# Layer 3's aggregate of a graph network on one core: groups of eight tiles and a ring of 32 gathers

## The chip, the core and the metric

The kernel runs on one core of a Trainium2 chip. The core has TensorE (PE, matrix products; its weight loads are listed as PEld), VectorE (DVE), ScalarE (ACT), GpSimd (POOL) and SyncE (SP), each with a program of its own; they meet only through semaphores. The metric is the time on the device of one execution of the whole kernel, in microseconds. TensorE's clock has two levels, 1.2 and 2.4 GHz; the profile gives the granted clock as a share of the upper one.

## The reference

The model has four layers, each with a graph part and a feed-forward part, on 3125 nodes with 256 features and 50000 edges. The change touches the graph part of the last layer:

```python
def _L3_gnn_ref(node_repr, weight, bias, edge_index, edge_types):
    h_all = jnp.einsum('ni,roi->rno', node_repr, weight)      # 8 relations
    src, dst = (edge_index[0], edge_index[1])
    msgs = h_all[edge_types, src]                             # 50000 rows of 256
    messages = jax.ops.segment_sum(msgs, dst, num_segments=node_repr.shape[0])
    return messages + bias
...
x = x + _L3_gnn_ref(_layernorm(x, axis=-1), L3_gnn_weight, L3_gnn_bias, edge_index, edge_type_8)
x = x + _L3_ffn_ref(_layernorm(x, axis=-1)[None], ...)
```

## The kernel before

A stage ahead of this one has written `h_all` as a table of 8 x 3125 rows to HBM (`g.relations`), and the edges have been sorted by their destination and cut into ST = 416 tiles of 128 edges, so that all edges of a tile go to nodes of one block of 125 (there are T = 25 blocks). The tile's block number is in `g.kmap`; an edge's row in the table and its place in the block are in `g.slots`. The sum over edges of tile n is then

- a gather (GpSimd, line 915): 128 rows of 1 KB of the table to `got[:, n % 16, :]`, an indirect DMA whose landing counts the semaphore `gathered[n % 16]` up by 16;
- a one-hot matrix (VectorE, line 935): 128 edges by 125 places, made for four tiles at a time (`QUAD`), written to `hot`, with the semaphore `hot_ready`;
- a product (TensorE, line 928): `hot` turned, times `got`, 125 x 256 values in one half of a PSUM bank. It stands as two records in the trace. Every second tile counts `multiplied` up;
- an addition (VectorE, line 954) of the product to the block's rows of X, whose place is a register loaded from `g.kmap`. Every second tile counts `added` up.

The order on each engine is that of the loops over n. GpSimd has 16 places: from gather 16 on, it waits ahead of every second gather for `multiplied` of the tiles 16 places back. TensorE waits for each gather's landing, for the one-hots of its four tiles, and from tile 16 on for `added`, since PSUM holds 16 products (8 banks of two). VectorE makes the one-hots of tiles n+8 to n+11 before it adds the products of tiles n to n+3, and waits for `multiplied` ahead of each addition. ScalarE has turned the indices into integers before the first gather, and SyncE has nothing to do, since the list `loads` is empty.

The stage stands by itself between two barriers in which all semaphores that are free are cleared. Behind it follows the last feed-forward part (`layer3_ffn`, lines 2376 to 2608), which reads X.

In the printed order of instructions semaphores have the first name that their number was given: same_loaded0 is `multiplied`, same_loaded1 is `added`, deg_opened is `hot_ready`, deg_hot_used is `staged`, and moved0 to moved15 are `gathered`. In the same way the profile calls a wait for number 141 (`multiplied`) sometimes by an early DMA, edges_other, that used the number first.

## Time and profile before

| | us |
|---|---|
| median of 3 runs | 4360.08 (4359.11 to 4368.43) |
| the profiled execution | 4384.73 |
| its span, first to last instruction | 4383.0 |
| the stage of the change, 3349.2 to 3950.2 us of the span: GpSimd busy | 405.1, 416 gathers |
| TensorE busy in it | 341.7, 832 records |
| VectorE busy in it | 175.5 for 416 additions, 70.6 for 104 one-hots |

The rows further down come from the views of this profile. A row of instructions reads: line, engine, operation, what is written <- what is read, shapes, count, busy time and mean, and behind a second bar the idle time of the engine ahead of them with what ended it. "issue" means that the profile shows nothing that the engine waited for.

### The profile page before, as it was taken

To read this page: it belongs to the slowest core of one execution; us is meant where nothing else is said; L and a number is where in the kernel's file an instruction comes from. 1 tells how busy PE (TensorE), PEld (TensorE's weight loads), DVE (VectorE), ACT (ScalarE), POOL (GpSimd) and SP (SyncE) were. 2 spreads that over 40 slices of the span, in tenths; PEclk is the share of its full clock that TensorE was granted. 3 is DMA by queue.
4 is the path that set the end of the run, shared out by engine and by line. 5 is a ranking of instruction groups with operands and counts; after the bars stand their busy time and mean duration, and the time that the engine had idled before them with its cause. 6 is when DMAs were issued, how large, how long until landed. Compare 5 with 4: busy or idle time off the path is not lost. (4 is left out here: it accounts for less than half of the span.)

```text
span 4383.0 us, 52512 instructions
## 1 busy us (share of the span) xinstructions
PE 3195.9 (73%) x17915; PEld 2449.1 (56%) x17916; DVE 1390.7 (32%) x3307; ACT 804.2 (18%) x2090; POOL 2275.9 (52%) x1830
## 2 busy tenths in 40 slices
PE   0999955574999993596089999968697555553993
PEld 0555543454999993596078878855443333332562
DVE  3333355442441114011621111133432434442005
ACT  0666622211000001232121100023200000001220
POOL 5587777775666666765236656600002666662003
PEclk9999977777999995798599999969897666665996
DMA  8663222228999886699133333300143333332222
GB/s 338 233 191 84 4 6 6 11 8 246 276 286 276 253 233 156 156 245 228 42 127 133 134 119 131 107 15 0 39 140 123 91 91 92 93 90 75 98 90 69
DMA packets 368093, 562.71 MB, mean 128 GB/s; under 512 B 177053, under 2 KB 246493, under 8 KB 351584
## 3 DMA queue, kind: packets, MB, share of 16 engines
q1 hardware_dynamic: 201740, 393.74, 28.0%
q0 software_dynamic: 158320, 122.06, 15.2%
q10 hardware_dynamic: 7824, 44.20, 2.5%
q8 instruction: 122, 2.00, 0.2%
q14 instruction: 87, 0.71, 0.0%
HBM read 413.40 MB, written 145.88 MB: 128 GB/s over the span
## 5 line engine op out<-in xcount | busy, mean ns | idle before, releaser
L455 POOL DMA_INDIRECT count_cells<-cells_count,added_row x391 | 645.4, 1651 | 282.8 <-issue 119.4
L874 POOL DMA_INDIRECT weight_cells<-added_weight,added_row x391 | 610.2, 1561 | 321.2 <-DMA weight_cells<-added_weight,added_row 181.4
L915 POOL DMA_INDIRECT g3g_got<-relations,g3g_idx x416 | 405.1, 974 | 685.7 <-ACTq L86 498.2
L1429 PE MATMUL g_acc<-XN,g_blocks 125*125 125x128 f32 x5000 | 567.8, 275 | 55.0 <-DMA g_blocks<-count_cells 52.6
L1429 PEld LDWEIGHTS g_acc<-XN,g_blocks 125*125 125x125 f32 x5000 | 559.6, 189 | 59.6 <-issue 52.8
L1742 PE MATMUL g_acc<-g_H,g_blocks 125*125 125x256 f32 x2500 | 557.6, 382 | 23.8 <-DMA g_blocks<-weight_cells 13.2
L1659 POOL DMA_INDIRECT slots_dram<-sort_rec,sort_row x392 | 379.8, 969 | 349.0 <-issue 112.5
L928 PE MATMUL g3g_pp<-g3g_got,g3g_hot 128*125 128x256 f32 x832 | 341.7, 560 | 271.4 <-issue 205.8
L1742 PEld LDWEIGHTS g_acc<-g_H,g_blocks 125*125 125x125 f32 x2500 | 471.4, 189 | 102.5 <-issue 31.8
L928 PEld LDWEIGHTS g3g_pp<-g3g_got,g3g_hot 128*125 128x125 f32 x832 | 203.8, 270 | 409.5 <-issue 247.8
L954 DVE TENSOR_TENSOR X<-X,g3g_pp 125x256 f32 x416 | 175.5, 422 | 349.2 <-DMA edges_other<-digits_dram 183.7
L723 ACT ACTIVATE same_same<-same_scores 128x128 bf16<-128x128 f32 (+7 forms) x392 | 255.1, 651 | 145.5 <-PE same_scores L712 129.0
L708 PE MATMUL same_scores<-edges_other,edges_own 11*128 11x512 bf16 (+2 forms) x490 | 206.9, 483 | 22.5 <-ACT same_same L723 21.5
L1786 DVE SCALAR_TENSOR_TENSOR g_tmp<-g_acc,dinv,g_b 125x256 f32<-125x256 f32 x50 | 24.2, 484 | 506.8 <-PE g_acc L1742 250.6
L2582 POOL DMA_INDIRECT f3y_Y<-results,f_back x25 | 35.6, 1426 | 273.7 <-PEq L86 266.3
L1869 PE MATMUL g_psO<-g_w,g_xT 128*125 128x512 f32 x400 | 173.8, 596 | 0.0
L1450 ACT ACTIVATE g_uT<-g_psT 128x125 f32<-128x125 f32 (+1 forms) x75 | 20.6, 275 | 627.3 <-PE g_psT L1404 528.7
L2117 PEld LDWEIGHTS f1e_pH<-XN,f1e_w 128*128 128x128 f32 x1040 | 128.2, 194 | 3.8 <-issue 0.4
L2139 PE MATMUL f1e_pY<-w,XN 128*128 x512 | 123.0, 384 | 10.0 <-issue 10.0
L2117 PE MATMUL f1e_pH<-XN,f1e_w 128*128 128x128 f32 x1040 | 128.5, 278 | 0.0
L1869 PEld LDWEIGHTS g_psO<-g_w,g_xT 128*125 128x125 f32 x400 | 75.4, 189 | 94.9 <-issue 94.9
L710 PE MATMUL same_scores<-edges_other,edges_own 11*128 11x128 bf16 x392 | 119.9, 306 | 8.1 <-DMA edges_other<-digits_dram 8.1
(624 smaller groups left out, 4530.4 us busy)
## 6 DMA issues: line engine op xcount, KB each, us to landing
g_blocks<-count_cells SPq DMA_DIRECT2D x500, 312.5 KB
g_blocks<-weight_cells SPq DMA_DIRECT2D x50, 1562.5 KB
count_cells<-edges_stripe ACTq DMA_DIRECT2D x25, 1562.5 KB
weight_cells<-edges_stripe POOLq DMA_DIRECT2D x25, 1562.5 KB
f1e_w<-in_L_ffn_w SPq DMA_DIRECT2D x68, 512.0 KB
relations<-g_ys SPq DMA_DIRECT2D x25, 896.0 KB
f_w<-in_L_ffn_w SPq DMA_DIRECT2D x16, 1024.0 KB, 9.9
bins<-zeros SPq DMA_DIRECT2D x1, 8704.0 KB, 32.8
```

The source lines that it names most:

```text
L455: pool.indirect_dma_start(out=rows, out_offset=bass.IndirectOffsetOnAxis(ap=g.cell_row[:, t:t + 1], axis=0), in_=g.cell_count[:, t:t + 1], ...
L708: nc.tensor.matmul(self.scores[:, k % self.SCORES, lo:hi], own[:, j, n:n + 128], other[:, j, lo:hi], start=True, stop=True)
L723: self.nc.scalar.activation(self.same[:, k % self.SAME, 0:n], self.scores[:, k % self.SCORES, 0:n], ACT.Relu, accum_out=self.found[:, k:k ...
L874: pool.indirect_dma_start(out=rows, out_offset=bass.IndirectOffsetOnAxis(ap=g.cell_row[:, t:t + 1], axis=0), in_=g.cell_weight[:, t:t + 1] ...
L915: pool.indirect_dma_start(out=got[:, j, :], out_offset=None, in_=table[:, :], in_offset=bass.IndirectOffsetOnAxis(ap=idx[:, n:n + 1], axis ...
L928: last = nc.tensor.matmul(pp[0:P, n // 2 % BANKS, half], hot[:, j, :], got[:, j, :], start=True, stop=True)
L954: last = nc.vector.tensor_tensor(part, part, pp[0:P, n // 2 % BANKS, half], ALU.add)
L1429: last = nc.tensor.matmul(acc[0:P, i % ACCS, 0:128], blocks[0:P, i % BLOCKS, t * P:(t + 1) * P], rhs[p][:, t, :], start=(t == 0), stop=(t ...
L1659: pool.indirect_dma_start(out=g.slots_dram[:, :], out_offset=bass.IndirectOffsetOnAxis(ap=self.row[:, c:c + 1], axis=0), in_=self.rec[:, c ...
L1742: last = nc.tensor.matmul(acc[0:P, i % 3, 0:D], blocks[0:P, i % BLOCKS, t * P:(t + 1) * P], H[p][0:P, t, :], start=(t == 0), stop=(t == T ...
L1869: last = nc.tensor.matmul(psO[0:P, c, :], xT[:, j, k, :], w[:, k, 2 * c:2 * c + 2, :].rearrange("p r n -> p (r n)"), start=(k == 0), stop= ...
L2117: last = nc.tensor.matmul(pH[:, j % 2, f * 128:(f + 1) * 128], w1[:, j % AHEAD, k, f * 128:(f + 1) * 128], xT[:, j % 2, k * 128:(k + 1) * ...
```

## The change

`aggregate` works in groups of eight tiles. The ring of gathers and of one-hots has 32 places. A group's eight landings count up one semaphore (four in turn, by 128 a group), TensorE waits once for a group's landings, one-hots and PSUM half, makes eight products, and counts `multiplied` up once. VectorE makes one-hots for eight tiles in one instruction, loads eight block numbers, waits once, adds eight times and counts `added` up once. GpSimd waits, from gather 32 on and ahead of every eighth, for `added` of the group four back. PSUM has the same 16 places, as two halves of eight. The empty loop of SyncE is gone.

```diff
-    QUAD, BANKS = 4, 8
+    EIGHT, RING, BANKS = 8, 32, 8
+    GROUPS = ST // EIGHT
...
-        got = sb("got", [128, R, width])
-        hot = sb("hot", [128, R, P])
-        pp = ps("pp", [128, BANKS, 512])
+        got = sb("got", [128, RING, width])
+        hot = sb("hot", [128, RING, P])
+        pp = ps("pp", [128, 2, EIGHT, width])
...
-        before = [g.count(j, 16 * (ST // R)) - 16 * (ST // R) for j in range(R)]
+        SETS = RING // EIGHT
+        gathered = g.moved[0:SETS]
+        landed = [g.count(i % SETS, 16 * EIGHT) for i in range(GROUPS)]
...
             for n in range(ST):
-                j = n % R
-                if n >= R and n % 2 == 0:
-                    pool.wait_ge(multiplied, (n - R) // 2 + 1)
-                pool.indirect_dma_start(out=got[:, j, :], out_offset=None, in_=table[:, :],
+                if n >= RING and n % EIGHT == 0:
+                    pool.wait_ge(added, (n - RING) // EIGHT + 1)
+                pool.indirect_dma_start(out=got[:, n % RING, :], out_offset=None, in_=table[:, :],
                                         in_offset=bass.IndirectOffsetOnAxis(ap=idx[:, n:n + 1], axis=0)
-                                        ).then_inc(gathered[j], 16)
+                                        ).then_inc(gathered[n // EIGHT % SETS], 16)
 
         @block.tensor
         def _(pe):
-            for n in range(ST):
-                j = n % R
-                pe.wait_ge(gathered[j], 16 * (n // R + 1) + before[j])
-                pe.wait_ge(hot_ready, n // QUAD + 1)
-                half = slice(n % 2 * width, (n % 2 + 1) * width)
-                if n % 2 == 0 and n >= 2 * BANKS:
-                    pe.wait_ge(added, n // 2 - BANKS + 1)
-                last = nc.tensor.matmul(pp[0:P, n // 2 % BANKS, half], hot[:, j, :], got[:, j, :], start=True, stop=True)
-                if n % 2 == 1:
-                    last.then_inc(multiplied, 1)
+            for i in range(GROUPS):
+                pe.wait_ge(hot_ready, i + 1)
+                if i >= 2:
+                    pe.wait_ge(added, i - 1)
+                pe.wait_ge(gathered[i % SETS], landed[i])
+                for m in range(EIGHT):
+                    n = i * EIGHT + m
+                    last = nc.tensor.matmul(pp[0:P, i % 2, m, :], hot[:, n % RING, :], got[:, n % RING, :], start=True, stop=True)
+                last.then_inc(multiplied, 1)
...
+            one_hots(1)
+            for i in range(GROUPS):
+                if i + 2 < GROUPS:
+                    one_hots(i + 2)
+                keys = load_keys(nc, mybir.EngineType.DVE, g.kmap, i * EIGHT, EIGHT, T)
+                dve.wait_ge(multiplied, i + 1)
+                for m in range(EIGHT):
+                    dve.drain()
+                    part = row(acc, keys[m], 0, width)
+                    last = nc.vector.tensor_tensor(part, part, pp[0:P, i % 2, m, :], ALU.add)
+                last.then_inc(added, 1)
```

GpSimd's instructions at the head of the stage, before: sixteen gathers, and then a wait for `multiplied` ahead of every second.

```order
L915 DMA g3g_got<-relations,g3g_idx 128x256 [waits deg_hot_used]
L915 DMA g3g_got<-relations,g3g_idx 128x256 x15
L915 DMA g3g_got<-relations,g3g_idx 128x256 [waits same_loaded0]
L915 DMA g3g_got<-relations,g3g_idx 128x256
L915 DMA g3g_got<-relations,g3g_idx 128x256 [waits same_loaded0]
L915 DMA g3g_got<-relations,g3g_idx 128x256
```

And with the change:

```order
L909 DMA g3g_got<-relations,g3g_idx 128x256 [waits deg_hot_used]
L909 DMA g3g_got<-relations,g3g_idx 128x256 x31
L909 DMA g3g_got<-relations,g3g_idx 128x256 [waits same_loaded1]
L909 DMA g3g_got<-relations,g3g_idx 128x256 x7
L909 DMA g3g_got<-relations,g3g_idx 128x256 [waits same_loaded1]
```

The first wait for room stands behind 32 gathers instead of 16, it is for another engine's semaphore, and seven gathers follow each without one. TensorE's instructions from the ninth pair of tiles on, before:

```order
L928 MATMUL g3g_pp<-g3g_got,g3g_hot 125x256 [waits deg_opened,moved15]
L928 MATMUL g3g_pp<-g3g_got,g3g_hot 125x256 [waits same_loaded1,deg_opened,moved0]
L928 MATMUL g3g_pp<-g3g_got,g3g_hot 125x256 [waits deg_opened,moved1]
L928 MATMUL g3g_pp<-g3g_got,g3g_hot 125x256 [waits same_loaded1,deg_opened,moved2]
L928 MATMUL g3g_pp<-g3g_got,g3g_hot 125x256 [waits deg_opened,moved3]
```

And with the change, from the first group on:

```order
L922 MATMUL g3g_pp<-g3g_got,g3g_hot 125x256 [waits moved0,deg_opened]
L922 MATMUL g3g_pp<-g3g_got,g3g_hot 125x256 x7
L922 MATMUL g3g_pp<-g3g_got,g3g_hot 125x256 [waits moved1,deg_opened]
L922 MATMUL g3g_pp<-g3g_got,g3g_hot 125x256 x7
L922 MATMUL g3g_pp<-g3g_got,g3g_hot 125x256 [waits moved2,same_loaded1,deg_opened]
L922 MATMUL g3g_pp<-g3g_got,g3g_hot 125x256 x7
```

Each tile had a wait of its own; now one product in eight has. From the third group on, its wait includes `added` of the group two back.

## Rows read from the trace of the kernel before

**Rows 1.** The page's costliest groups: the gathers

```profile
L915 POOL DMA_INDIRECT g3g_got<-relations,g3g_idx x416 | 405.1, 974 | 685.7 <-ACTq L86 498.2
```

**Rows 2.** The view of line 915: least, median and longest duration in ns

```profile
L915 POOL DMA_INDIRECT g3g_got<-relations,g3g_idx x416: 941/949/1452, 3349.2 to 3940.8; - x139
```

**Rows 3.** Timeline at the stage's end: start, duration, engine, operation, idle before

```profile
3940.82 0.95 POOL L915 DMA_INDIRECT g3g_got<-relations,g3g_idx  x1 [0.30 <-issue]
...
3947.81 0.49 PEld L928 LDWEIGHTS g3g_pp<-g3g_got,g3g_hot 128*125 128x125 f32 x2 [0.84 <-DMA g3g_got<-relations,g3g_idx]
...
3949.78 0.42 DVE L954 TENSOR_TENSOR X<-X,g3g_pp 125x256 f32 x1 [0.18 <-issue]
```

**Rows 4.** Timeline of GpSimd, the first and last of 14 gathers in a row

```profile
3464.02 0.95 POOL L915 DMA_INDIRECT g3g_got<-relations,g3g_idx  x1 [0.30 <-issue]
...
3480.30 0.95 POOL L915 DMA_INDIRECT g3g_got<-relations,g3g_idx  x1 [0.30 <-PE g3g_pp L928]
```

**Rows 5.** The view of waits in the stage: total us, times, longest

```profile
POOL g3g_got L915 <- issue: 111.5, 361, 0.8
...
POOL g3g_got L915 <- DMA edges_other<-digits_dram: 63.6, 34, 4.0
POOL g3g_got L915 <- PE g3g_pp L928: 12.4, 20, 2.6
```

**Rows 6.** Windows, line 928 and then line 954: busy and count in the stretch

```profile
3340.00:3375.20 35.20, 20.98 (x37) 9.36 (x38) 0.52 0.34 102
```

```profile
3340.00:3392.00 52.00, 6.75 (x16) 0.54 0.34 101
```

**Rows 7.** Timeline from 3371 to 3399 us, some rows of each engine

```profile
3371.67 0.42 DVE L954 TENSOR_TENSOR X<-X,g3g_pp 125x256 f32 x1 [1.79 <-DMA edges_other<-digits_dram]
...
3382.89 0.42 DVE L954 TENSOR_TENSOR X<-X,g3g_pp 125x256 f32 x1 [10.20 <-PE g3g_pp L928]
...
3384.69 3.75 PE L928 MATMUL g3g_pp<-g3g_got,g3g_hot 128*125 128x256 f32 x8 [2.17 <-issue]
...
3388.55 0.95 POOL L915 DMA_INDIRECT g3g_got<-relations,g3g_idx  x1 [0.30 <-issue]
3392.02 0.42 DVE L954 TENSOR_TENSOR X<-X,g3g_pp 125x256 f32 x1 [7.43 <-DMA edges_other<-digits_dram]
3392.15 0.95 POOL L915 DMA_INDIRECT g3g_got<-relations,g3g_idx  x1 [2.65 <-DMA edges_other<-digits_dram]
...
3398.76 0.76 PE L928 MATMUL g3g_pp<-g3g_got,g3g_hot 128*125 128x256 f32 x1 [10.32 <-issue]
```

**Rows 8.** Timeline of the first tiles, and a lone tile later

```profile
3350.52 0.97 POOL L915 DMA_INDIRECT g3g_got<-relations,g3g_idx  x1 [0.30 <-issue]
...
3353.35 0.49 PEld L928 LDWEIGHTS g3g_pp<-g3g_got,g3g_hot 128*125 128x125 f32 x2 [0.78 <-DMA g3g_got<-relations,g3g_idx]
...
3354.71 0.42 DVE L954 TENSOR_TENSOR X<-X,g3g_pp 125x256 f32 x1 [4.78 <-PE g3g_pp L928]
...
3417.23 1.22 PE L928 MATMUL g3g_pp<-g3g_got,g3g_hot 128*125 128x256 f32 x2 [0.94 <-DMA g3g_got<-relations,g3g_idx]
```

**Rows 9.** Timeline of a burst of eight tiles, and two one-hots four tiles apart

```profile
3616.23 6.08 PE L928 MATMUL g3g_pp<-g3g_got,g3g_hot 128*125 128x256 f32 x16 [10.14 <-issue]
...
3618.57 0.68 DVE L935 TENSOR_TENSOR g3g_hot<-iota,slots 128x500 f32<-128x500 f32 x1
...
3621.69 0.68 DVE L935 TENSOR_TENSOR g3g_hot<-iota,slots 128x500 f32<-128x500 f32 x1
```

**Rows 10.** Timeline: a gather and a one-hot that meet, twice

```profile
3358.07 0.95 POOL L915 DMA_INDIRECT g3g_got<-relations,g3g_idx  x1 [0.30 <-issue]
3358.26 0.68 DVE L935 TENSOR_TENSOR g3g_hot<-iota,slots 128x500 f32<-128x500 f32 x1
...
3418.47 0.68 DVE L935 TENSOR_TENSOR g3g_hot<-iota,slots 128x500 f32<-128x500 f32 x1 [0.97 <-issue]
3418.59 1.38 POOL L915 DMA_INDIRECT g3g_got<-relations,g3g_idx  x1 [0.30 <-issue]
```

More of the change, by code:

```diff
@@ L888, in aggregate @@
         idx = sb("idx", [128, ST], I32)
-        got = sb("got", [128, R, width])
-        hot = sb("hot", [128, R, P])
-        pp = ps("pp", [128, BANKS, 512])
+        got = sb("got", [128, RING, width])
+        hot = sb("hot", [128, RING, P])
+        pp = ps("pp", [128, 2, EIGHT, width])
         staged, hot_ready, multiplied, added = sem("staged"), sem("hot_ready"), sem("multiplied"), sem("added")
-        gathered = g.moved
-        before = [g.count(j, 16 * (ST // R)) - 16 * (ST // R) for j in range(R)]
+        SETS = RING // EIGHT
+        gathered = g.moved[0:SETS]
+        landed = [g.count(i % SETS, 16 * EIGHT) for i in range(GROUPS)]
         block = ctx.enter_context(stage(nc, g))
-        @block.sync
-        def _(sp):
-            for k, load in enumerate(loads):
-                sp.wait_ge(multiplied, ST * (2 * k + 1) // (2 * len(loads)))
-                load(sp)
         @block.scalar
@@ L932, in one_hots @@
-        def one_hots(n):
-            m = min(QUAD, ST - n)
-            nc.vector.tensor_tensor(hot[:, n % R:n % R + m, :], wide(g.iota[:, 0:P], 128, m, P),
-                                    g.slots[:, n:n + m, 1:2].broadcast_to([128, m, P]), ALU.is_equal).then_inc(hot_ready, 1)
+            for i in range(GROUPS):
[7 more added lines that the diff above has]
+                last.then_inc(multiplied, 1)
@@ L938, in _, with one_hots @@
+        def one_hots(i):
+            places = slice(i * EIGHT % RING, i * EIGHT % RING + EIGHT)
+            nc.vector.tensor_tensor(hot[:, places, :], wide(g.iota[:, 0:P], 128, EIGHT, P),
+                                    g.slots[:, i * EIGHT:(i + 1) * EIGHT, 1:2].broadcast_to([128, EIGHT, P]),
+                                    ALU.is_equal).then_inc(hot_ready, 1)
         @block.vector
@@ L940, in _ @@
             one_hots(0)
-            one_hots(QUAD)
-            for n in range(ST):
-                if n % QUAD == 0:
-                    keys = load_keys(nc, mybir.EngineType.DVE, g.kmap, n, QUAD, T)
-                    if n + 2 * QUAD < ST:
-                        if n >= 2 * QUAD:
-                            dve.wait_ge(multiplied, (n - QUAD) // 2)
-                        one_hots(n + 2 * QUAD)
-                dve.drain()
-                half = slice(n % 2 * width, (n % 2 + 1) * width)
-                dve.wait_ge(multiplied, n // 2 + 1)
-                part = row(acc, keys[n % QUAD], 0, width)
-                last = nc.vector.tensor_tensor(part, part, pp[0:P, n // 2 % BANKS, half], ALU.add)
-                if n % 2 == 1:
-                    last.then_inc(added, 1)
+            one_hots(1)
[9 more added lines that the diff above has]
+                last.then_inc(added, 1)
 def store(nc, g, tag, dram, src, width, done=None, value=16):
```

## The prediction, made before the changed kernel was timed

> **What bounds the kernel now.** The page first: the profiled execution took 4384.7 us, of which 4383.0 us is the span, against a median of 4360.1 us; differences are worked out in the profiled execution and taken over to the median as they are. The change touches one stage only, layer 3's aggregate, lines 881 to 956. The view of one line [rows 2] gives its extent: 416 gathers, the first started at 3349.2 us and the last at 3940.8 us, and the last addition ends at 3949.78 + 0.42 = 3950.2 us [rows 3]. The stage is 601.0 us long, and all that follows waits for it behind a barrier, so a microsecond gained or lost here is one of the whole.
>
> Which engine bounds it? GpSimd issues the gathers one behind the other. Between 3464.02 and 3480.30 us are 13 undisturbed steps [rows 4]: 16.28/13 = 1.2525 us each, 0.949 of it the gather itself (the median in [rows 2]) and 0.30 issue. 415 such steps are 519.8 us; the real ones took 3940.8 - 3349.2 = 591.6. The missing 71.8 us have two sources. The waits of GpSimd [rows 5]: 34 that the view puts down to a DMA and 20 to TensorE are 63.6 + 12.4 = 76.0 us, less the usual 54 x 0.30, so 59.8 us. And long gathers: 405.1 us busy [rows 1] less 416 x 0.949 = 394.8 leaves 10.3 us. The remaining 1.7 us are slightly long issue gaps.
>
> What are the 54 waits? The order of GpSimd's instructions names the semaphore: same_loaded0, which is `multiplied`. (The view names an early DMA because the number was that DMA's before; it was long done.) So GpSimd's ring of 16 is full and waits for TensorE's signal. But TensorE is not late with its work. In the stretch before 3375.2 us it had begun 37 records, two to a tile, so 18 tiles [rows 6], while VectorE had made only 16 additions by 3392 us; its 17th starts at 3392.02 after 7.43 us of idle time, and GpSimd starts again at 3392.15 [rows 7]. The 37th record had begun, so the 18th tile, whose signal this addition needs, was through 16.8 us earlier, and TensorE's last burst before the addition ended at 3384.69 + 3.75 = 3388.4 us. Both waiters come free at once: the signal came late, not the work. In the first tiles it did not: TensorE began its second tile, which closes the first pair, at 3353.35, a lone tile takes 1.22 us, and the addition starts at 3354.71, 0.14 us behind its end [rows 8]. Later waits of VectorE end 11.2 and 9.1 us apart (3371.67, 3382.89, 3392.02) [rows 7]. TensorE then starves in turn, 10.32 us until 3398.76, because the one-hots it needs stand behind VectorE's wait.
>
> **The change part by part.**
>
> 1. Room. The ring goes from 16 to 32 gathers. In steady flow GpSimd can begin group i+4 when group i is added; it takes 4 x 8 x 1.2525 = 40.1 us to get there. What must fit into it: the issue of group i up to its last gather's start (7 x 1.2525 = 8.8 us), that gather's landing (2.8 us from its start to its tile, 3350.52 to 3353.35 in [rows 8]), TensorE's eight tiles (16 records; 6.08 us for 16 in [rows 9], but 16 x 0.427 = 6.8 us when none is at the fast clock, by the pace (3.75 - 0.76)/7 of the eight records in [rows 7]), the signal, and VectorE's adds. VectorE handles four tiles and one one-hot in 3.12 us [rows 9], so twice that less 0.15 for the one longer one-hot (part 3), 6.1 us for a group. Without the signal that is 8.8 + 2.8 + 6.8 + 6.1 = 24.5 us, so a signal up to 15 us late costs GpSimd nothing by this count. I take the 59.8 us as gone. Bounds: nothing of it gone, or all.
>
> 2. Signals. TensorE gives 52 instead of 208, VectorE 52 of `added` instead of 208, and TensorE waits for 52 groups of landings instead of 416 gathers. By themselves I count them at nothing: no row shows a signal's own price. The Trainium skill, "TensorE: Matmul & The Clock Gate", section "The cost: per-tile semaphore tail", gives about 26 ns for each increment, so by it 156 fewer would save some 4 us as an estimate and a signal would never be 17 us late; [rows 7] contradict the second, and the measurement decides.
>
> 3. One-hots. 52 of 128x1000 replace 104 of 128x500. The latter take 0.68 us [rows 10], an addition of 256 values 0.42, so (0.68 - 0.42)/244 = 1.07 ns a value and 1.21 us for the new one (twice 0.68 is the upper end, 1.36). On VectorE this hides: 6.1 us of work for 10.0 us of gathers. But it holds up GpSimd. A one-hot begun at 3418.47 lets the gather begun at 3418.59 take 1.38 us instead of 0.95, 0.43 us more; the one begun at 3358.26, after the gather's 3358.07, costs nothing [rows 10]. So a gather whose start falls into a one-hot is held until the one-hot ends. Spread evenly, each new one costs 1.21²/(2 x 1.2525) = 0.58 us, 52 of them 30 us. The same formula gives 0.68²/2.505 x 104 = 19.2 us for before, of which 10.3 were measured; by that ratio 16 us. Ends: 10 us as before and 52 x 1.21 = 63 us, if the group rhythm puts every one-hot right ahead of a gather. I take 23 us, between 16 and 30. The Trainium skill, "SBUF — State Buffer", section "Who interferes with whom", speaks against this edit: a VectorE instruction with two SBUF inputs and a GpSimd instruction that reads SBUF hold each other off for their whole length. [rows 10] agree in the first direction and not in the second, since the one-hot at 3358.26 began in the middle of a gather; by the page GpSimd's 23 us would be the same, and VectorE would lose up to 0.95 us a group, which stays hidden.
>
> 4. The tail. Before, tiles trickle through and 9.4 us lie between the last gather's start and the end. Now the last group is one burst: the last gather's tile can begin 3947.81 - 3940.82 = 7.0 us after its issue [rows 3], where landings are slow, and then come eight tiles (6.8 us at the slow clock), 0.15 us for the signal, and eight additions (seven steps of 0.61 and 0.42, 4.7 us). 18.6 us, 9.2 more than before. The lower end is 3.4 us less, with the tiles at the fast clock, twice the slow one; a signal 10 us late would be on top.
>
> 5. SyncE's empty loop and the first wait for a whole group go beside gathers that are being issued anyway: nothing.
>
> Sum: 519.8 + 23 + 18.6 = 561.4 us for the stage instead of 601.0, 39.6 us less. 4384.7 - 39.6 = 4345.1 in a profiled execution, 4360.1 - 39.6 = 4320.5 us as a median.
>
> **The rivals.**
>
> The late signal becomes a period (slower). PSUM now holds two groups, and TensorE may begin group i+2 only when group i is added. In that loop stand 6.8 us of tiles, the lateness L of the one signal, and 6.1 us of VectorE; two groups of gathers with their holds take 20.9 us. From L = 8.0 on the loop is the longer one. Before, TensorE had the same 16 tiles of PSUM, but given back by pairs, so that 17 us of lateness just fitted. With L = 10.5, about the distance of the waits' ends in [rows 7], a group takes 11.7 us: 11.6 to the first landing, 51 x 11.7, and 22 for the last group give 630 us, 29 more, so 4389 us. L = 9.4 is the break-even against 601 us; with L = 17 it is 802 us and 4561. For it: [rows 7] show the lateness while TensorE waits for landings, as it will between bursts. Against it: it was absent in [rows 8] in the same pattern, and with a quarter of the signals none queues behind another.
>
> Half of the waits stay. GpSimd now waits for `added`, which comes a whole group of additions after the product, instead of for `multiplied`; if 30 us of the 59.8 come back, 4350 us. For it: the wait is at a later point of the chain. Against: it has 32 places.
>
> The one-hots fall into step with the gathers. Eight gathers and one one-hot are one period, so what is hit once is hit each time; at the upper end of 63 us the gain is gone: 4360 us. Against it: TensorE's bursts alternate between its clocks, so the phase wanders.
>
> **How the numbers follow.** The forecast of 4320 us gets 0.55, with its own range of 4295 to 4340 (holds of 10 to 40 us, the tail at either clock). The late signal 0.22, half of the waits 0.13, the one-hots in step 0.10. A measurement here can tell about 0.2% from no change, 8.7 us. Faster: nearly all of the forecast, half of the second rival and some of the third, 0.60. Within 0.2%: 0.14. Slower: the late signal and a part of the others, 0.26. The range of 4292 to 4405 takes in the late signal up to L of about 11.
>
> **What would show it.** Right: the gathers' first to last start falls from 591.6 to about 543 us, and GpSimd's waits other than issue to a few us; the additions in runs of eight, each run starting within 1 us after a burst; gathers of 1.2 to 2.1 us, about one to a group, with a mean of about 1.00 us instead of 0.974. The tail about 18 us. Wrong: bursts of TensorE more than 10.5 us apart with VectorE idle between a burst's end and its additions for 8 us or more (the first rival), GpSimd waiting once per group for an addition (the second), or the mean of a gather at 1.1 us (the third).

## The result: 1.2% slower, and the profile after

The changed kernel takes 4412.24 us (median of 4 runs, 4406.96 to 4416.74) against 4359.59 us (4353.49 to 4368.43) of the kernel before beside it: ratio 1.0116, 95% interval 1.0096 to 1.0135. The forecast was 4320.5 us, the range ended at 4405: the time lies outside it and on the other side. The profiled execution took 4410.65 us with a span of 4408.9.

The stage now runs from 3341.5 us to 3974.68 + 0.42 = 3975.1 us, 633.6 us instead of 601.0 and instead of the 561.4 forecast. First the page's row for the gathers and the view of their line (answering [rows 1, 2]):

```profile
L909 POOL DMA_INDIRECT g3g_got<-relations,g3g_idx x416 | 425.9, 1024 | 690.9 <-ACTq L86 500.7
```

```profile
L909 POOL DMA_INDIRECT g3g_got<-relations,g3g_idx x416: 942/949/1992, 3341.5 to 3956.6; - x139
```

Busy time is 425.9 us, so 425.9 - 394.8 = 31.1 us lie in long gathers, 10.3 before. From the first to the last start it is 615.1 us, 591.6 before. The view of waits (total us, times, longest) answers to [rows 5]:

```profile
POOL g3g_got L909 <- issue: 122.2, 401, 0.3
...
POOL g3g_got L909 <- DVE X L944: 67.9, 14, 11.3
...
DVE X L944 <- DMA edges_other<-digits_dram: 222.9, 11, 30.8
...
DVE X L944 <- PE g3g_pp L922: 86.3, 15, 16.4
```

Of GpSimd's 14 waits for an addition seven are longer than 0.3 us, about 9 us each; less the usual issue the 14 are 63.7 us, against 59.8 in 54 waits before. So the waits did not go; they were gathered into seven. VectorE waited up to 30.8 us at a time (again the view names an early DMA whose semaphore number is now TensorE's signal). One such place, in the timeline, answers to [rows 7]:

```profile
3364.58 1.19 DVE L928 TENSOR_TENSOR g3g_hot<-iota,slots 128x1000 f32<-128x1000 f32 x1
...
3364.84 5.34 PE L922 MATMUL g3g_pp<-g3g_got,g3g_hot 128*125 128x256 f32 x16 [5.15 <-DMA g3g_got<-relations,g3g_idx]
3365.13 1.46 POOL L909 DMA_INDIRECT g3g_got<-relations,g3g_idx  x1 [0.30 <-issue]
...
3374.79 5.38 PE L922 MATMUL g3g_pp<-g3g_got,g3g_hot 128*125 128x256 f32 x16 [4.60 <-DMA g3g_got<-relations,g3g_idx]
...
3391.98 0.95 POOL L909 DMA_INDIRECT g3g_got<-relations,g3g_idx  x1 [0.30 <-issue]
3396.53 0.42 DVE L944 TENSOR_TENSOR X<-X,g3g_pp 125x256 f32 x1 [30.76 <-DMA edges_other<-digits_dram]
...
3401.17 4.17 PE L922 MATMUL g3g_pp<-g3g_got,g3g_hot 128*125 128x256 f32 x9 [21.01 <-DVE X L944]
3401.34 1.66 POOL L909 DMA_INDIRECT g3g_got<-relations,g3g_idx  x1 [8.41 <-DVE X L944]
```

TensorE's records of the second group end at 3364.84 + 5.34 = 3370.18 us; VectorE's first addition of it starts at 3396.53, 26.35 us later. In between GpSimd gathered without a break until 3391.98 + 0.95 = 3392.93, when its 32 places were full, and 3.6 us after that the signal was there. The trace has the count of `multiplied` itself at 3396.35, 0.18 us ahead of the addition: it was made late, and not heard late. The same happens in seven groups of 52, 24 to 30 us late each time, each ended 2 to 6.5 us after GpSimd had stopped. These seven are not the only late ones: in 17 of the 52 groups the first addition starts more than 8 us after the burst's records end. Seven more are the groups right behind (20 to 23 us, a part of it the additions of the group ahead of them), and three came 10 to 12 us late while GpSimd went on gathering. One of these three, whose burst's records end at 3431.09:

```profile
3442.78 0.95 POOL L909 DMA_INDIRECT g3g_got<-relations,g3g_idx  x1 [0.30 <-issue]
3443.03 0.42 DVE L944 TENSOR_TENSOR X<-X,g3g_pp 125x256 f32 x1 [12.65 <-issue]
...
3444.03 0.95 POOL L909 DMA_INDIRECT g3g_got<-relations,g3g_idx  x1 [0.30 <-issue]
```

So a late signal can also come while gathers stream. In the other groups TensorE and VectorE catch up, and many signals come 0.20 us after the burst. The earlier rows also show the price of a long one-hot: the gather begun at 3365.13, inside it, takes 1.46 us instead of 0.95. In the whole stage 49 gathers start inside a one-hot, and these hold all of the extra time; none of the other 367 takes over 0.97 us. The end of the stage, answering to [rows 3]:

```profile
3956.60 0.94 POOL L909 DMA_INDIRECT g3g_got<-relations,g3g_idx  x1 [0.30 <-issue]
...
3964.34 5.95 PE L922 MATMUL g3g_pp<-g3g_got,g3g_hot 128*125 128x256 f32 x16 [7.36 <-DMA g3g_got<-relations,g3g_idx]
...
3970.49 0.42 DVE L944 TENSOR_TENSOR X<-X,g3g_pp 125x256 f32 x1 [5.07 <-PE g3g_pp L922]
...
3974.68 0.42 DVE L944 TENSOR_TENSOR X<-X,g3g_pp 125x256 f32 x1 [0.17 <-issue]
```

3975.1 - 3956.6 = 18.5 us of tail, 9.4 before. Together: 519.8 of cadence + 63.7 of pauses + 31.1 of long gathers + 18.5 of tail = 633.1, and 0.5 of slightly long issue gaps.

### The profile page after: what moved, and what is told of

Same layout as the page of the kernel before. It is cut to its first block and busy times, and to the rows that moved or that the text cites. A ratio compares the mean times of both kernels' runs of the same rounds, so it can differ in the third digit from the quotient of the medians.

```text
span 4408.9 us, 52044 instructions
## 1 busy us (share of the span) xinstructions
PE 3138.8 (71%) x17915; PEld 2463.9 (56%) x17916; DVE 1377.0 (31%) x3255; ACT 803.9 (18%) x2090; POOL 2300.5 (52%) x1830
## 5 line engine op out<-in xcount | busy, mean ns | idle before, releaser
L909 POOL DMA_INDIRECT g3g_got<-relations,g3g_idx x416 | 425.9, 1024 | 690.9 <-ACTq L86 500.7
L922 PE MATMUL g3g_pp<-g3g_got,g3g_hot 128*125 128x256 f32 x832 | 283.7, 515 | 358.4 <-DMA g3g_got<-relations,g3g_idx 193.0
L922 PEld LDWEIGHTS g3g_pp<-g3g_got,g3g_hot 128*125 128x125 f32 x832 | 216.8, 267 | 425.8 <-issue 324.1
L708 PE MATMUL same_scores<-edges_other,edges_own 11*128 11x512 bf16 (+2 forms) x490 | 206.9, 483 | 22.5 <-ACT same_same L723 21.1
```

The source lines that it names most:

```text
L708: nc.tensor.matmul(self.scores[:, k % self.SCORES, lo:hi], own[:, j, n:n + 128], other[:, j, lo:hi], start=True, stop=True)
L909: pool.indirect_dma_start(out=got[:, n % RING, :], out_offset=None, in_=table[:, :], in_offset=bass.IndirectOffsetOnAxis(ap=idx[:, n:n + 1 ...
L922: last = nc.tensor.matmul(pp[0:P, i % 2, m, :], hot[:, n % RING, :], got[:, n % RING, :], start=True, stop=True)
```

## The experiments

Two kinds of occasion have to be told apart, since without that no number below can be read: the kernel before took 4360 to 4373 us beside the result and beside e9 to e11, e14 and e18, and 4279 to 4282 us beside the others. One chip showed both (number 12, beside e1 to e4 and e9 to e11). I call them *late* and *quiet*; every kernel is compared with the kernel before beside it. That time is a single execution for e14 and e18, and for e17 it is the one of e15 and e16. "Pauses" are GpSimd's gaps of over 0.6 us in the stage, less the usual issue (so 37 where the text above counts 54 waits), "long" the gathers' busy time above 416 x 0.949, "tail" the last gather's start to the stage's end, all in us and all from one profiled execution. A ratio is given where a kernel was timed several times.

| kernel | before beside it | its time | ratio, interval | stage | pauses | long | tail |
|---|---|---|---|---|---|---|---|
| before (late, first profile) | - | 4359.59 | | 601.0 | 59.9 in 37 | 10.3 | 9.4 |
| after (late) | 4359.59 | 4412.24 | 1.0116, 1.0096 to 1.0135 | 633.6 | 63.7 in 7 | 31.1 | 18.5 |
| e1 hardly any gathers (quiet) | 4281.91 | 4077.58 | | 335.2 | 0 | | |
| e2 ring of 16 (quiet) | 4281.91 | 4380.85 | 1.0233, 1.0216 to 1.0250 | 632.9 | 66.6 in 26 | 27.2 | 18.4 |
| e3 signal on a drain (quiet) | 4281.91 | 4307.66 | 1.0051, 1.0035 to 1.0068 | 561.0 | 0 | 22.5 | 18.1 |
| e4 landings by ScalarE (quiet) | 4281.91 | 4306.92 | 1.0051, 1.0034 to 1.0068 | 564.7 | 0 | 25.6 | 18.8 |
| e5 before again (quiet) | 4279.13 | 4279.32 | 0.9999, 0.9990 to 1.0009 | 538.1 | 0 | 7.8 | 10.1 |
| e6 after again (quiet) | 4279.13 | 4303.78 | 1.0054, 1.0037 to 1.0071 | 557.2 | 0 | 17.6 | 19.3 |
| e7 drain again (quiet) | 4279.13 | 4304.08 | 1.0059, 1.0042 to 1.0076 | 557.5 | 0 | 18.4 | 18.9 |
| e8 drain, halved one-hots (quiet) | 4279.13 | 4296.81 | 1.0037, 1.0023 to 1.0051 | 551.3 | 0 | 12.5 | 18.6 |
| e9 second listener (late) | 4367.86 | 4413.96 | | 639.4 | 72.2 in 7 | 28.6 | 18.4 |
| e10 halves and fine tail (late) | 4367.86 | 4409.64 | 1.0106, 1.0076 to 1.0136 | 636.6 | 81.6 in 8 | 21.1 | 13.6 |
| e11 before, ring of 32 (late) | 4367.86 | 4384.25 | 1.0039, 1.0027 to 1.0052 | 604.6 | 59.4 in 23 | 6.0 | 18.5 |
| e12 drain, third (quiet) | 4280.51 | 4302.55 | 1.0061, 1.0044 to 1.0078 | 558.0 | 0 | 19.1 | 18.7 |
| e13 relay, second (quiet) | 4280.51 | 4310.56 | | 561.5 | 0 | 22.6 | 18.7 |
| e14 two signals (late) | 4370.31 | 4408.78 | | 640.4 | 71.8 in 9 | 30.2 | 18.2 |
| e15 relay, third (quiet) | 4280.55 | 4297.01 | | 557.6 | 0 | 18.4 | 19.0 |
| e16 halves and fine tail (quiet) | 4280.55 | 4287.27 | 1.0020, 1.0010 to 1.0030 | 542.7 | 0 | 11.5 | 10.9 |
| e17 relay, fourth (quiet) | 4280.55 | 4307.91 | | 564.1 | 0 | 24.7 | 19.2 |
| e18 relay, fifth (late) | 4372.77 | 4415.27 | | 646.3 | 73.5 in 7 | 26.0 | 26.5 |

**First experiments: four ways to free the signal.** e1 gathers only the first 32 tiles and multiplies those places again and again (the rest of the gathers is left out):

```
...
-            for n in range(ST):
+            for n in range(RING):
...
-                pe.wait_ge(gathered[i % SETS], landed[i])
+                if i < SETS:
+                    pe.wait_ge(gathered[i % SETS], landed[i])
```

> The changed kernel, with only the first 32 of the 416 gathers; the other tiles are multiplied from the rows that lie in the ring, so layer 3's sums are wrong by what is left out. Theory S (TensorE's signal is held back while gathers flow): without them each signal arrives within 0.5 us after the burst, VectorE's additions follow at once, and the stage takes 52 times what the slower of TensorE (3.7 to 6.8 us a group) and VectorE (5.9 us) needs, 310 to 370 us instead of 633.6. Rival L (the lateness belongs to TensorE and VectorE's hand-over itself, to waiting for `added` or to one signal per eight tiles): lateness of 10 us or more goes on after the first four groups, 10 us or more a group, and the stage takes over 520 us.

e2 gathers into 16 places and keeps the 32 of the one-hots:

```
-    EIGHT, RING, BANKS = 8, 32, 8
+    EIGHT, RING, HOTS, BANKS = 8, 16, 32, 8
...
```

> The changed kernel with a ring of 16 gathers instead of 32 (the one-hots keep their 32 places). GpSimd then waits for `added` of the group two back: 8.8 us of issue, 2.8 to the tile, 5.4 of TensorE, 0.2, 5 of VectorE are 22.2 us for each 20.0 us of issue, so GpSimd must pause some 2 to 3 us per group or two. Theory S (the signals come when GpSimd pauses): frequent short pauses let them through, no signal is later than about 10 us, and the stage takes 590 to 640 us, so 4370 to 4420 in all: half the ring costs little or nothing against the changed kernel's 4412. Rival R (the ring is what absorbs a signal late by itself, 20 us and more): two groups then take over 40 us whenever a signal is late, and with 17 of 52 late ones the stage takes over 750 us, 4530 or more in all.

e3 puts the signal on a drain behind the group's last matmul:

```
-                last.then_inc(multiplied, 1)
+                pe.drain().then_inc(multiplied, 1)
```

> The changed kernel, with `multiplied` counted up by TensorE's queue after a drain instead of by the last product of a group. If it is the products' own way of signalling that is held back, the signals arrive within 1 us, GpSimd's seven pauses (63.7 us) go, and the stage takes 519.8 + 31 + 18.5 = 569 us, 4348 in all. Theory S in its general form (anything that TensorE sends is held back while gathers flow): no change, 4400 to 4425, lateness of 20 to 30 us as before.

e4 lets ScalarE wait for each group's landings and tell TensorE:

```
...
+            for i in range(GROUPS):
+                hold(act, gathered[i % SETS], landed[i], told)
...
-                pe.wait_ge(gathered[i % SETS], landed[i])
+                pe.wait_ge(told, i + 1)
```

> The changed kernel, with ScalarE waiting for the landings of each group and telling TensorE by a semaphore of its own, so that TensorE never waits for a semaphore that DMAs count up. If TensorE's signals are held back by its own wait for such a semaphore, they now come at once and the kernel takes 4348 us. Theory S: no change beyond the 0.1 us or so of the relay, 4400 to 4425, with the same lateness of 20 to 30 us.

No signal was late in any of the four, also not in e2, where nothing about the signal had been changed. e3's stage of 561.0 us looked like a cure, but the kernel before was 78 us faster beside it than beside the result. So the missing lateness could be the occasion's, and none of the four decides between its theories. e2 is of use by itself: with prompt signals, a ring of two groups makes GpSimd wait 26 times, 66.6/26 = 2.6 us each, so the chain from a group's first gather to its last addition is 20.0 + 2.6 = 22.6 us without held gathers. Read directly, with them, it is 23.4 us as a mean of the 52 groups; the prediction had 24.5. Its wait row (total us with the usual issue in it):

```profile
  DVE X L944: 76.7, 32
```

**Second: is it the kernel or the occasion?** Before and after unchanged, e3 again, and e3 with one-hots in halves, four tiles each:

```
...
-            places = slice(i * EIGHT % RING, i * EIGHT % RING + EIGHT)
+            places = slice(i * 4 % RING, i * 4 % RING + 4)
...
-                if i + 2 < GROUPS:
-                    one_hots(i + 2)
+                if i + 2 < GROUPS:
+                    one_hots(2 * i + 4)
...
                 for m in range(EIGHT):
+                    if m == 4 and i + 2 < GROUPS:
+                        one_hots(2 * i + 5)
...
```

> The kernel before, unchanged, profiled on the chip that the three other kernels of this call run on. Theory C (the waits are a matter of the chip or the hour, not of the kernel): where this kernel takes about 4280 us, its aggregate of layer 3 shows hardly a pause of GpSimd (stage about 541 us = 519.8 of cadence + 10 of long gathers + 9 of tail); where it takes about 4360, 55 to 65 us of pauses as in [rows 5], and a stage near 601. Rival: the 78 us between the two measurements lie in other stages, and the stage is 601 us at 4280 too.

> The kernel after, unchanged, beside the others on the same chip. Theory C: without late signals on this chip it has a stage of 561 to 565 us and takes 4305 to 4310 us beside 4282 before; its first additions follow TensorE's bursts by about 0.2 us. Theory S (the late signal belongs to this kernel's signal on a matmul, and drain or relay took it away): seven pauses of about 9 us, a stage of 625 to 640 us, 4370 to 4385 us, on whatever chip.

> After with TensorE's signal on a drain, once more, on one chip with after. Theory C: the same as after within 2 us if this chip has no late signals; if it has them, late here too (stage 620 or more). Theory S: a stage of 561 us, 60 to 75 us below after's.

> After with the signal on a drain and the one-hots written as 128x500, two instructions per group, the second after the fourth addition; else as the drain kernel. Theory O (the double-width one-hot is what holds gathers): the time in long gathers falls from 22 to 25 us to the 10 us that [rows 7] had, the stage to 549 us, 12 to 14 us below the drain kernel, about 4294 beside 4282. Rival (it is the total one-hot time that collides, however cut): 22 to 25 us stay, and the time is the drain kernel's within 3 us.

Theory C held in e5, e6 and e7, with e6's stage 4 us below its range. The view of the gathers' line, first e5 and then e6:

```profile
L915 POOL DMA_INDIRECT g3g_got<-relations,g3g_idx x416: 942/946/1433, 3304.9 to 3832.9; - x139
...
  issue: 114.8, 377
  PE g3g_pp L928: 11.6, 38
...
DMA to landing us min/median/max: 2.7/2.8/7.6
```

```profile
L909 POOL DMA_INDIRECT g3g_got<-relations,g3g_idx x416: 942/946/1988, 3309.5 to 3847.4; - x139
...
  issue: 126.4, 415
```

The 34 waits put down to a DMA in [rows 5] are not there for the kernel before either, and its 38 "PE" waits are 0.3 us each, plain issue. So on a quiet occasion the room that the change adds is worth nothing, and what it costs stands alone: the stage goes from 538.1 to 557.2 us, 19.1 more, of which 17.6 - 7.8 = 9.8 are long gathers and 19.3 - 10.1 = 9.2 tail. The time rises by 24.7 us; in the profiles 4.6 of it lie ahead of the stage, which no part of the change explains (the quiet profiles enter the stage anywhere from 3303.5 to 3315.5 us). After and drain differ by 0.3 us. Halved one-hots bring the long gathers from 18.4 to 12.5 us and the time down by 7.3, half of the 12 to 14 that I had expected: e7 had less to lose than e3, and the halves keep more than the kernel before. The longest gather falls from 1.99 us in the quiet profiles with one-hots of 128x1000 to 1.43, as in the kernel before. The page's rows of e6 and e8:

```profile
L909 POOL DMA_INDIRECT g3g_got<-relations,g3g_idx x416 | 412.4, 991 | 617.6 <-ACTq L86 491.2
```

```profile
L909 POOL DMA_INDIRECT g3g_got<-relations,g3g_idx x416 | 407.3, 979 | 619.6 <-ACTq L86 493.1
```

**Third: who sees the signal late?** This met a late occasion. e9 is after with ScalarE as a second listener:

```
+            for i in range(GROUPS):
+                act.wait_ge(multiplied, i + 1)
+                nc.scalar.copy(mark[0:1, i:i + 1], g.slots[0:1, i, 1:2])
```

> After, and beside VectorE also ScalarE waits for each group's signal and then copies one element. Where the chip has no late signals (before near 4280) both start within 0.5 us of the burst's end, and the time is after's 4304 within 8 us. Where it has them (before near 4360): theory T (TensorE sends the signal late, or it travels late), ScalarE starts as late as VectorE, 17 to 30 us after the burst; theory V (the signal is there, and VectorE's own start is held while GpSimd gathers), ScalarE starts within 0.5 us of the burst while VectorE is 17 to 30 us late.

Timeline of its eighth and ninth group, all engines but for GpSimd's even run of gathers, of which the last stands:

```profile
3433.07 6.74 PE L926 MATMUL g3g_pp<-g3g_got,g3g_hot 128*125 128x256 f32 x16 [3.48 <-DMA g3g_got<-relations,g3g_idx]
...
3443.40 6.69 PE L926 MATMUL g3g_pp<-g3g_got,g3g_hot 128*125 128x256 f32 x16 [3.59 <-DMA g3g_got<-relations,g3g_idx]
...
3460.49 0.94 POOL L913 DMA_INDIRECT g3g_got<-relations,g3g_idx  x1 [0.30 <-issue]
3467.01 0.35 ACT L905 COPY g3g_mark<-slots 1x1 f32<-1x1 f32 x2 [32.00 <-DMA edges_other<-digits_dram]
3467.17 0.42 DVE L948 TENSOR_TENSOR X<-X,g3g_pp 125x256 f32 x1 [26.55 <-DMA edges_other<-digits_dram]
```

The two bursts' records end at 3439.81 and 3450.09. ScalarE, which had nothing else to do, starts at 3467.01, with both of its copies in one go (x2), VectorE 0.16 us later. Theory V falls, T stands: the signal is late for both listeners, and the signals of both bursts come free together, 5.6 us after GpSimd's last gather ended.

e10 is after with halved one-hots and the last group in four pairs:

```
...
+        ends = [g.count(SETS + k, 32) for k in range(4)]
...
+                    if i == GROUPS - 1 and m % 2 == 0:
+                        pe.wait_ge(g.moved[SETS + m // 2], ends[m // 2])
...
+                    if m == EIGHT - 1 or (i == GROUPS - 1 and m % 2 == 1):
+                        last.then_inc(multiplied, 1)
...
```

> After with the one-hots in two halves per group (signal on the matmul as in after), and the last group in four pairs: their landings waited for by pairs, one signal per pair. Where the chip has no late signals: cadence 519.8, long gathers 12.5 as with halves before, the tail falls from 19.3 to before's 10 us, so a stage of 542 us, 4287 us beside 4280 before, ratio 1.002. Rival (the tail is not the group's width but the burst's clock): the tail stays 18 to 19 us and the time 4296. On a chip with late signals: 60 to 76 us more, the tail's answer read from the trace.

Long gathers and tail shrink (21.1 and 13.6 us), but the pauses are 81.6, and its ratio to before is after's within the intervals.

e11 is the kernel before with a ring of 32 gathers, landings waited for by pairs:

```
...
-                if n >= R and n % 2 == 0:
-                    pool.wait_ge(multiplied, (n - R) // 2 + 1)
+                if n >= RING and n % 2 == 0:
+                    pool.wait_ge(multiplied, (n - RING) // 2 + 1)
...
-                pe.wait_ge(gathered[j], 16 * (n // R + 1) + before[j])
+                if n % 2 == 0:
+                    pe.wait_ge(gathered[n // 2 % R], landed[n // 2])
...
```

> Before with pairs as they are, but a ring of 32 gathers in place of 16, and landings waited for by pairs. Where the chip has no late signals the ring is never full: the same as before within 3 us. Where it has them, theory S (a signal comes as late as GpSimd goes on gathering, whatever the ring): pauses of GpSimd of 50 to 70 us stay, fewer and longer, time within 15 us of before; rival (lateness is at most 19 us of its own, as [rows 5, 7] had it, and 32 gathers of 1.25 us cover it): no pauses, stage 541 us, 60 us below before.

Twice the room for gathers, with everything behind them as before but the pairs' common landing, gains nothing: 59.4 us of pauses in 23, 59.9 before. Theory S holds, also in the lateness itself: the latest signal is 41.5 us late with 32 places and 19.4 with the 16 of the kernel before. The time is 16 us above before, where the stage accounts for 3.6 (9.1 of tail among it); the rest isn't explained. Its additions in the first stretch, one row for each pair:

```profile
3369.37 0.42 DVE L955 TENSOR_TENSOR X<-X,g3g_pp 125x256 f32 x1 [6.21 <-PE g3g_pp L929]
...
3379.87 0.42 DVE L955 TENSOR_TENSOR X<-X,g3g_pp 125x256 f32 x1 [8.81 <-issue]
...
3390.37 0.42 DVE L955 TENSOR_TENSOR X<-X,g3g_pp 125x256 f32 x1 [9.36 <-DMA edges_other<-digits_dram]
...
3401.57 0.42 DVE L955 TENSOR_TENSOR X<-X,g3g_pp 125x256 f32 x1 [9.51 <-DMA edges_other<-digits_dram]
```

TensorE had finished these pairs by 3366 to 3373 us, 2.5 us apart. Their signals come 10.5 to 11.2 us apart, the fifth 37.0 and the sixth 41.5 us late, until the ring is full. So signals do come while gathers stream, but fewer than bursts are begun, and the lateness grows from one to the next: it is no fixed amount that a buffer covers.

**Later: does a drain or a relay help?** e12 and e13 are e3 and e4 again, and met a quiet occasion:

> After with TensorE's signal on a drain behind each group, asked where the late signals are at hand (before near 4360 in the same hour; where before is near 4280 this run is a repetition: 4304 to 4308). Theory H (what is held is the increment that a matmul carries): signals within 0.3 us of the burst, no pause of GpSimd, a stage of 557 to 561 us, so 4300 + the 32 to 44 us that other stages lose in such an hour, 4335 to 4352 us, below before. Rival K (any increment of TensorE is held while gathers stream): the same seven pauses, 64 to 72 us, and 4405 to 4415 us.

> After with the landings waited for by ScalarE and told to TensorE, asked beside it. Theory K2 (TensorE's signals are late because TensorE itself waits for a DMA's semaphore while gathers stream): prompt signals and no pause here where after's own are late, 4335 to 4352 us; rival (who waits for the landing has no part in it): seven pauses, 4405 to 4415 us. Where before is near 4280: 4300 to 4308.

They take 4302.55 and 4310.56 us, within 3 us of what was expected there, and say nothing of the question. e14 therefore carries both signals at once, so that a single late run could tell:

```
-                last.then_inc(multiplied, 1)
+                last.then_inc(matmul_done, 1)
+                pe.drain().then_inc(multiplied, 1)
...
+                act.wait_ge(matmul_done, i + 1)
```

> After with two signals of TensorE per group: the last matmul's own increment, for which only ScalarE waits (and then copies one element), and behind it a drain whose increment VectorE waits for. Where before is near 4360: theory H (the matmul's increment is held, the drain's isn't), ScalarE starts 17 to 30 us late in some groups and VectorE within 0.5 us, 4335 to 4352 us; theory K (every increment of TensorE is held while gathers stream), both late in the same seven or eight groups, 4405 to 4420 us; theory H2 (the drain frees both), neither late. Where before is near 4280 neither is late, and it takes 4300 to 4310 us.

It met one. Timeline of the second group; GpSimd's last gather before its pause stands for the run of them:

```profile
3356.07 5.12 PE L927 MATMUL g3g_pp<-g3g_got,g3g_hot 128*125 128x256 f32 x16 [5.21 <-DMA g3g_got<-relations,g3g_idx]
...
3383.34 0.95 POOL L914 DMA_INDIRECT g3g_got<-relations,g3g_idx  x1 [0.30 <-issue]
3387.79 0.19 ACT L906 COPY g3g_mark<-slots 1x1 f32<-1x1 f32 x1 [36.24 <-remote]
...
3388.66 0.42 DVE L950 TENSOR_TENSOR X<-X,g3g_pp 125x256 f32 x1 [31.45 <-PEq L929]
3388.68 5.88 PE L927 MATMUL g3g_pp<-g3g_got,g3g_hot 128*125 128x256 f32 x16 [27.49 <-issue]
```

The matmul's own signal is seen 26.6 us after the records end, the drain's 27.5. The trace has the drain itself as lasting 32.34 us, from 3356.13 to 3388.47, where those of groups with prompt signals last 3.5 to 6.7; TensorE takes up the next group only behind it. Nine pauses, 4408.78 us and both signals late is theory K as it was worded (it had seven or eight pauses): every increment of TensorE comes late, the drain's too. I read it as TensorE not coming to the end of its burst. That the records end at 3361.19 does not contradict this, since matmul ends in the profile are modelled; but a burst that is done and whose acknowledgement or count is held would look the same, also to a drain that waits for it. The Trainium skill, "Perfetto Trace Analysis", section "Tensor Engine Instruction (MATMUL, LD_WEIGHTS)", says the same of them, and that the semaphore is updated only after PSUM has acknowledged all bytes; the trace agrees in so far as the drain's end (3388.47) and ScalarE's start (3387.79) lie 0.7 us apart, and no run here shows which of the two steps is the late one.

The same profile shows how far GpSimd's stop counts. In its 32nd group GpSimd stopped 9.6 us after the records' end, and the first addition is only 13.4 us behind it, 3.8 us after the stop. In its 29th the records end at 3687.47, and ScalarE starts at 3708.38 and VectorE at 3709.96, in the middle of an unbroken run of gathers. So a stop of GpSimd is mostly what ends a long lateness, but not always.

> After with each group's landings waited for by ScalarE and told to TensorE. Where before is near 4360 to 4370: theory K (TensorE's matmuls come to their end late while gathers stream, whoever waits for the landings), seven to nine pauses, 64 to 72 us, 4405 to 4415 us; theory K2 (it is TensorE's own wait for a DMA's semaphore), no pause and 4335 to 4352 us. Where before is near 4280: 4300 to 4311 us as twice before.

> After with the landings waited for by ScalarE and told to TensorE, asked for an occasion with late bursts. Where before is near 4360 to 4370: theory K (matmuls end late while gathers stream, whoever waits for the landings), seven to nine pauses, 64 to 72 us, 4405 to 4415 us; theory K2 (it is TensorE's own wait for a DMA's semaphore), no pause and 4335 to 4352 us. Where before is near 4280 it repeats 4297 to 4311 us and tells nothing of this.

> The relay kernel once more, as in the expectation before this one: where before is near 4360 to 4370, theory K gives seven to nine pauses and 4405 to 4415 us, theory K2 none and 4335 to 4352; where before is near 4280, it repeats 4297 to 4311 us and tells nothing of this.

The relay met quiet occasions in e15 and e17 (4297.01 and 4307.91 us). In e18 it met a late one and took 4415.27 us beside 4372.77: seven pauses, 73.5 us, each behind a burst 26 to 29 us late, and one more such burst behind the last gather, which makes the tail 26.5 us. Who waits for the landings has no part in it.

> After with halved one-hots and the last group in four pairs, once more. Where before is near 4280: no pauses, cadence 519.8, long gathers 12.5 as with halves alone, a tail of 13.6 us as this kernel had it, so a stage of 546 us and 4288 us, ratio 1.002. Rival (halves and tail don't add up, as the additions of the last pairs trail): 551 us and 4297. Where before is near 4360: as measured, ratio 1.0106.

e16 is e10's kernel on a quiet occasion: 4287.27 us, ratio 1.0020, where 4288 was expected. That the time fits so well is in part luck, since the stage was to be 546 us with a tail of 13.6. Its last pair, timeline:

```profile
3840.01 0.95 POOL L910 DMA_INDIRECT g3g_got<-relations,g3g_idx  x1 [0.30 <-issue]
...
3847.68 2.07 PE L926 MATMUL g3g_pp<-g3g_got,g3g_hot 128*125 128x256 f32 x4 [1.78 <-DMA g3g_got<-relations,g3g_idx]
...
3850.53 0.42 DVE L953 TENSOR_TENSOR X<-X,g3g_pp 125x256 f32 x1 [0.17 <-issue]
```

3850.95 - 3840.0 = 10.9 us of tail. The stage is 542.7 us, of 557.2 in e6, and what is left above before's 538.1 is 3.7 of long gathers and 0.8 of tail. No version beat the kernel before, late or quiet.

## Why the prediction was wrong

**Room (the step that failed).** "I take the 59.8 us as gone": 63.7 us were there. The count under it was fair, as e2 shows (23.4 us of chain, I had 24.5, so about 17 us of room for a late signal). What failed was to take the lateness of some 17 us in [rows 7] as a quantity that more room covers. It is a state that mostly lasts until GpSimd stops; with 32 places GpSimd stops later, so the signals that it waits for are 24 to 30 us late, and in e11 up to 41.5. [rows 7] had the hint, since VectorE came free when GpSimd had already stood for 2.5 us, and I read it as two waiters freed by one signal. Why TensorE's signals are late on some occasions stays open. The lower bound of the term, "nothing of it gone", was the case, but it carried only the second rival's 4350 us.

**Signals.** Nothing, as said, is not contradicted: in e6 the stage closes within 0.5 us (519.8 + 17.6 + 19.3 = 556.7 of 557.2) without such a term. But this is a sum of GpSimd's time, on which TensorE's prompt signals do not stand, so no run here measures the price of a signal, and the 26 ns of the Trainium skill ("TensorE: Matmul & The Clock Gate", section "The cost: per-tile semaphore tail") are neither borne out nor refuted. That figure would not foresee 24 to 30 us.

**One-hots.** 23 us taken, between 16 and 30; 31.1 in the profiled execution, 8.1 us too low there and just outside, and 17.6 to 25.6 with whole one-hots on quiet occasions. That the width does it, e8 and e16 show (12.5 and 11.5 us). One of 128x1000 lasts 1.19 us in the median, 1.21 forecast. The rule of the Trainium skill ("SBUF — State Buffer", section "Who interferes with whom") agrees in the direction that costs: the gather begun at 3365.13, inside a one-hot, took 0.51 us more. It does not agree in the other: the 20 one-hots of this profile that begin in the middle of a gather last 1.19 us like the rest.

**Tail.** 18.6 forecast, 18.5 measured, 9.1 more than before. e16 takes it back.

**Sum.** 561.4 was forecast and 633.6 came: 63.7 for the room, 8.1 for long gathers, 0.4 for the rest. On a quiet occasion the stage is 557.2 us in e6, near the forecast, but that is luck: there the kernel before has 538.1, without the 59.8 us. The gain was counted from an execution whose waits belong to the occasion, while the costs (parts 3 and 4) belong to the kernel: +24.7 us quiet. The profiled executions differ by 25.9 us (32.6 in the stage, less 7.7 by which after enters it earlier, and 1.0 behind it) and the medians by 52.7; the kernel before's own profiled execution lay 25.1 above its median and after's 1.6 below. Taking the profiled difference over to the median, as the first paragraph of the prediction does, was thus off by 26.7 us, a second step that failed. Why the kernel before is faster in its median runs stays open.

**The rivals.** "The late signal becomes a period" named the right place, TensorE's signal, and the right sign, 4389 us, with 0.22. It had the wrong form: a loop of TensorE and VectorE, one late signal for each group. The sign that was named for it did show, VectorE idle for 8 us or more behind ten of the 52 bursts, but only seven of them made GpSimd wait: these are seven fillings of the ring, and the pauses stand on GpSimd. Half of the waits: all came back, though not by the later point of the chain; e6 has none. The one-hots in step: 31.1 us, not 63.

## What to carry to other kernels

Before a wait is counted as gained by more buffers, ask what ends it: where the late signal mostly comes just after the waiting engine stops, the buffer only sets how long each wait is, not what they sum to (59.9, 63.7 and 59.4 us with 16, 32 and 32 places). A wait whose releaser had finished long before should be looked for in a second profile from another occasion, before it becomes a term of a sum. And where the wait is not the structure's own, coarser groups still pay their price, here 9 us at the end and 10 us in longer instructions that hold back the engine that sets the pace.

## What the runs showed of the hardware that was not expected

- On late occasions many of TensorE's signals come late while GpSimd streams gathers of 1.25 us: 24 to 30 us in seven groups of 52, ended 2 to 6.5 us after the last gather, and 10 to 12 us in three more, in the middle of the stream. A drain behind such a burst lasts 32.34 us instead of 3.5 to 6.7 (e14). With a signal for each pair and 32 places they come 10.5 to 11.2 us apart (e11). On quiet occasions, with the same instructions, the signals that VectorE waits for are seen 0.14 to 0.57 us after the records.
- What makes an occasion late is not shown. The gathers' transfers are as fast: each sends 16 count packets of 4 bytes, and the last of them ends 2.42 us after the gather's start in the median, in the late and in the quiet profile of the kernel before; and one chip was both. One thing does set the seven late profiles apart from the thirteen quiet ones: their record of semaphore counts has holes. Of the stage's 6656 counts by landed gathers they hold 1270 to 2371, the quiet ones every one (e1, with 32 gathers, all its 512). Whatever holds TensorE's signals may also hold the records, or the recording may itself be what holds TensorE; no run here separates the two, so whether the kernel is late when nothing is recorded stays open.
- On late occasions the pauses come back however the work is cut: 59.4 to 81.6 us in the seven late profiles, of seven kernels.
- The late profiles also enter this stage later: at 3330.8 to 3349.2 us, the quiet ones at 3303.5 to 3315.5.
